# Attention of layers 0 and 2: projections one head group further ahead, in two banks, with a single score bank and a ring of six for q

## The reference

```
x = x + tanh(g_xattn[i]) * xattn_i(layernorm(x), ctx)
x = x + tanh(g_ffn[i])   * ffn_i(layernorm(x))

# xattn of layers 0 and 2, 16 heads of 8:
q = xn @ Wq + bq;  k, v = ctx @ Wk + bk, ctx @ Wv + bv
attn = softmax(q @ k.T * scale  (+ mask * -1e9 in layer 2))
out  = (attn @ v) @ Wo + bo
```

## Time and profile before

| | |
|---|---|
| median of 3 runs | 1286.11 us (1279.64 to 1290.08) |
| the profiled execution | 1285.64 us, span 1283.9 us |
| TensorE busy | 977.4 us, 76% of the span |
| VectorE busy | 771.4 us, 60% |
| ScalarE busy | 571.7 us, 45% |
| GpSimd busy | 393.6 us, 31% |
| mean granted TensorE clock | 0.842 |
| batches of layer 0's attention | about 38 to 125 us of the span |
| batches of layer 2's attention | about 840 to 952 us |

### The profile page before, as it was taken

How to read it: one execution, slowest core, us unless ns; L and a number is a source line. 1 busy time by engine, 2 the same in 40 slices (tenths; PEclk the granted TensorE clock), 3 DMA queues, 4 the chain that set the end, 5 groups by cost and what they waited for, 6 DMA issues and landing times. The chain is left out here.

```text
span 1283.9 us, 17163 instructions
## 1 busy us (share of the span) xinstructions
PE 977.4 (76%) x5366; PEld 731.0 (57%) x5366; DVE 771.4 (60%) x1924; ACT 571.7 (45%) x1101; POOL 393.6 (31%) x519
## 2 busy tenths in 40 slices
PE   2797576698888888488888888478867578883766
PEld 2575354566566665266666666357745357772544
DVE  3687565566766777366666656356765414545674
ACT  1575242355555555155555544156634133321553
POOL 2432002122323232146565656333310132210321
PEclk9899677667777778689999999689978679996887
DMA  4000000000000000000000000100000200000001
GB/s 117 1 2 2 1 1 19 1 18 18 18 18 18 18 9 10 1 1 1 1 1 1 1 1 1 36 1 2 2 19 1 64 2 1 1 1 1 1 1 33
DMA packets 25607, 14.12 MB, mean 11 GB/s; under 512 B 10776, under 2 KB 25007, under 8 KB 25391
## 3 DMA queue, kind: packets, MB, share of 16 engines
q1 hardware_dynamic: 25518, 13.03, 3.8%
HBM read 11.98 MB, written 1.05 MB: 10 GB/s over the span
## 5 line engine op out<-in xcount | busy, mean ns | idle before, releaser
L1470 POOL TENSOR_TENSOR L1f_h<-L1f_h,L1f_gb 128x512 f32<-128x512 f32 (+1 forms) x96 | 152.2, 1588 | 116.5 <-DVE L1f_h L1760 96.7
L718 ACT ACTIVATE L_pt<-bank 128x512 f32<-128x512 f32 x224 | 131.3, 597 | 60.8 <-PE bank L604 56.9
L705 ACT ACTIVATE L_part<-bank,L_bias_ca,const 128x256 fp32r<-128x256 f32 x128 | 68.9, 563 | 111.9 <-PE bank L545 111.9
L406 POOL TENSOR_TENSOR L_kc<-L_kc_all,const 128x256 fp32r<-128x256 f32 x96 | 59.0, 618 | 179.7 <-PE bank L604 127.1
L1760 DVE TENSOR_TENSOR L1f_h<-L1f_a,bank 128x512 f32<-128x512 f32 (+1 forms) x96 | 65.4, 682 | 69.9 <-ACT L1f_a L1600 69.3
L1600 ACT ACTIVATE L1f_a<-bank 128x512 f32<-128x512 f32 (+1 forms) x96 | 57.3, 597 | 111.9 <-PE bank L1525 111.8
L1768 DVE TENSOR_TENSOR L1f_h_lo<-L1f_h,L1f_h_hi 128x512 fp32r<-128x512 f32 (+1 forms) x96 | 88.2, 919 | 11.1 <-ACT L1f_h_hi L1613 11.1
L844 DVE TENSOR_REDUCE L_ms<-bank 128x2 f32<-128x512 f32 x128 | 84.5, 687 | 17.0 <-PE bank L566 16.7
L566 PE MATMUL bank<-L_k,L_q 32*128 32x256 f32 x256 | 73.4, 397 | 12.2 <-DVE L_ms L844 8.9
L830 DVE SCALAR_TENSOR_TENSOR L_q<-bank,L_bias_c,L_part 128x256 fp32r<-128x256 f32 x96 | 46.2, 481 | 58.9 <-ACT L_part L705 57.7
L842 DVE TENSOR_REDUCE L_mc<-bank 128x8 f32<-128x512 f32 (+1 forms) x96 | 65.4, 682 | 24.2 <-PE bank L559 14.8
(11 more groups left out here) (405 smaller groups left out, 2608.9 us busy)
## 6 DMA issues: line engine op xcount, KB each, us to landing
L_raw<-in_L_ffn_w_dram SPq DMA_DIRECT2D x8, 176.0 KB, 2.3
L_raw<-in_L_ffn_v_dram SPq DMA_DIRECT2D x8, 176.0 KB, 2.5
const<-in_const_dram SPq DMA_DIRECT2D x1, 1036.0 KB, 5.0
x<-in_x_dram SPq DMA_DIRECT2D x2, 512.0 KB
L_raw<-in_L_ffn_w_dram SPq DMA_DIRECT2D x8, 128.0 KB, 2.6
L_mask<-in_mask_Bx1xSxS_ff_dram SPq DMA_DIRECT2D x2, 512.0 KB
out_dram<-x SPq DMA_DIRECT2D x2, 512.0 KB
L_raw<-in_L_ffn_w_dram SPq DMA_DIRECT2D x8, 48.0 KB, 2.5
```

What stands on the lines that cost most here:

```text
L705: last = act.activation(part[:, i].bitcast(F32R), b_proj[:, i * S:(i + 1) * S], ACT.Identity, bias=bias_ca[:, i, g:g + 1], scale=pr.c("ak" ...
L718: act.activation(pt[:, g // 2, (g % 2) * NS + i], b_st[(g * NS + i) % 2][:], ACT.Exp, scale=scale).then_inc(sem["exp_done"], 1)
L1470: pool.tensor_tensor(h[0:m, r], h[0:m, r], gb[0:m, gate_slot(c)], ALU.mult).then_inc(sem["h_done"], 1)
```

## The change

For layers 0 and 2 (not `own_keys`):

- `proj` is issued for group g+4 in place of g+3, and alternates between bank 0 and bank 3 (`proj_banks[g % 2]`). It waits for DVE L830 of two groups before, no longer of the group before. `part` is used in two halves in turn.
- Bank 3 was the second score bank. `scores` now has bank 2 alone and waits for the DVE maxima of the group before.
- `q` grows from four slots to a ring of six.
- `scale` and `turn` are issued for batch b+2 in group 3, where they were issued for b+1 in group 0. In `end[3]` the turn stands behind `y(b-1)`. `keys`, `mask_in` and `mask` stay in their places.
- `first` takes on the projection of group 3, `scale(1)` and `turn(1)`.

```diff
-        q = sb("q", [P, NG, S], F32R)
+        RING = NG if own_keys else NG + 2
+        q = sb("q", [P, RING, S], F32R)
+        proj_banks = (b_proj,) if own_keys else (b_proj, b_sc[1])
+        sc_banks = b_sc if own_keys else b_sc[:1]
+        AHEAD = len(proj_banks)
+        def slot(b, g):
+            return (b * NG + g) % RING
 ...
-            + banks("scores", 0, 1) + [("maxima", 0, 0)]
+            + banks("scores", 0, 1) + ([] if own_keys else [("proj", 0, 3), ("scale", 1)]) + [("maxima", 0, 0)] \
+            + ([] if own_keys else [("turn", 1)])
 ...
             if more:
-                begin[0] += [("scale", b + 1), ("mask_in", b + 1)]
-                end[0] += [("turn", b + 1)]
+                if own_keys:
+                    begin[0] += [("scale", b + 1)]
+                    end[0] += [("turn", b + 1)]
+                begin[0] += [("mask_in", b + 1)]
                 end[1] += [("mask", b + 1)]
             if late:
                 ...
                 end[3] += [("y", b - 1)]
+            if not own_keys and b + 2 < B:
+                begin[3] += [("scale", b + 2)]
+                end[3] += [("turn", b + 2)]
 ...
-                for at in group(g + 3):
-                    steps += [("proj", *at), ("keys", *at)]
+                steps += [("proj", *at) for at in (group(g + 3) if own_keys else group(g + 4))]
+                steps += [("keys", *at) for at in group(g + 3)]
 ...
 def proj (TensorE)
-                    need(pe, sem["qk_split"], b * NG + g)
+                    need(pe, sem["qk_split"], b * NG + g - (AHEAD - 1))
-                        o = b_proj[:, i * S:(i + 1) * S]
+                        o = proj_banks[g % AHEAD][:, i * S:(i + 1) * S]
 def scores (TensorE)
-                    need(pe, sem["sc_taken"], b * U + (at + i - 1))
-                    o = b_sc[(at + i) % 2]
+                    need(pe, sem["sc_taken"], b * U + (at + i - (len(sc_banks) - 1)))
+                    o = sc_banks[(at + i) % len(sc_banks)]
 def proj (VectorE)
-                    need(dve, sem["st_done"], b * U + (g + 1) * NS - U)
+                    need(dve, sem["st_done"], (b * NG + g + 1 - RING) * NS)
```

More of the change, by code:

```diff
@@ L558, in scores @@
                             ts = slice(t * P, (t + 1) * P)
-                            last = pe.matmul(o[:, t * S:(t + 1) * S], q[:, g, ts], kc[:, g], start=True, stop=not masked)
+                            last = pe.matmul(o[:, t * S:(t + 1) * S], q[:, slot(b, g), ts], kc[:, g], start=True, stop=not masked)
                             if masked:
@@ L595, in weights @@
                                 continue
-                            pe.matmul(op, keys_of, q[:, g], start=True, stop=False)
+                            pe.matmul(op, keys_of, q[:, slot(b, g)], start=True, stop=False)
                             if masked:
@@ L702, in proj @@
                     act.wait_ge(sem["proj_done"], b * NG + g + 1)
-                    need(act, sem["qk_split"], b * NG + g)
+                    need(act, sem["qk_split"], b * NG + g - (AHEAD - 1))
                     for i in range(2 if own_keys else 1):
-                        last = act.activation(part[:, i].bitcast(F32R), b_proj[:, i * S:(i + 1) * S], ACT.Identity,
+                        last = act.activation(part[:, i if own_keys else g % 2].bitcast(F32R), proj_banks[g % AHEAD][:, i * S:(i + 1) * S], ACT.Identity,
                                               bias=bias_ca[:, i, g:g + 1], scale=pr.c("ak" if i else "aq"))
@@ L827, in proj @@
                     dve.wait_ge(sem["proj_hi"], b * NG + g + 1)
-                    need(dve, sem["st_done"], b * U + (g + 1) * NS - U)
+                    need(dve, sem["st_done"], (b * NG + g + 1 - RING) * NS)
                     for i in range(2 if own_keys else 1):
-                        last = dve.scalar_tensor_tensor((k if i else q)[:, g], b_proj[:, i * S:(i + 1) * S], bias_c[:, i, g:g + 1],
-                                                        part[:, i], ALU.add, ALU.add)
+                        last = dve.scalar_tensor_tensor(k[:, g] if i else q[:, slot(b, g)], proj_banks[g % AHEAD][:, i * S:(i + 1) * S],
+                                                        bias_c[:, i, g:g + 1], part[:, i if own_keys else g % 2], ALU.add, ALU.add)
                     last.then_inc(sem["qk_split"], 1)
@@ L837, in scores @@
                     dve.wait_ge(sem["sc_done"], b * U + (at + i + 1))
-                    bank = b_sc[(at + i) % 2][:]
+                    bank = sc_banks[(at + i) % len(sc_banks)][:]
                     if i == 0:
```

## The result

The changed kernel took 1297.3 us (median of 20 runs, 1283.37 to 1305.81) against 1286.05 us (20 runs, 1269.41 to 1295.88): 11.25 us more. The ratio is 1.0091 with a 95% interval of [1.0063, 1.0119]; it is taken from the fast runs alone (16 of the 20 of the changed kernel), because some executions fall into a slower state. Forecast were 1293 us, or +7.4 on 1285.6, a ratio of 1.0058, in a range of 1282 to 1302. The time lies in the range, on the forecast side and within 1%; the size was too small by some 4 us.

What follows compares the result with a forecast made beforehand. Layer 0 batches were taken as near DVE's 8.30 us floor, layer 2 as paced by TensorE. Moved turns +4.05 and +3.9, edges +0.1 and -0.7, gave +7.4 on 1285.64: 1293 us, range 1282 to 1302.

Steps and rivals of the forecast that it cites:

- deciding term: Turn behind y waits for DVE's L902: +0.81 us per batch in layer 0, +0.78 in layer 2, five times each.
- DVE's account: 8.30 busy: Layer 0 batch counted on DVE: 8.30 busy + 0.51 + 0.34 + 0.13 + 1.03 of waits = 10.31 us.
- the walk: Step-by-step timing of one changed layer 0 batch from the end of `xt_lo`: 10.34 us, against 9.53 before.
- the wait of 0.13 before a second q: Layer 0, group 1: DVE was to wait 0.13 us before that group's q.
- The clock rival: Clock falls at the ten turns, one group at half rate after each: 10 us, 1303; two groups, 1313; 18%.
- signs of being wrong: L526 not waiting for L902, a layer 0 batch under 9.5 us, or the batches' clock column below 0.95.
- the main case: The walked case, with the turn waiting for y and granted clock still 1.00: 1289 to 1298 us, 63%.
- The sum: Layers 0 and 2 together: 4.05 + 3.9 + 0.1 - 0.7 = +7.4 us.
- The term for the edges: First and last batches of layers 0 and 2: +0.1 at the starts, -0.3 and -0.4 at the ends.
- The hidden turn: L902 as early as TensorE's y, turn starts at once: batches 9.31 and 12.5, -2 us, 1284; 14%.
- both waits vanish: Removed waits count fully, 0.8 + 0.66 us per layer 0 batch, 0.65 per layer 2 batch: -15, 1271; 5%.
- The part costed at nothing: Single score bank, other banks, ring and halves of `part`: no cost in the steady batches.

Runs made afterwards that it cites:

- e1: Changed kernel with y(b-1) moved behind the turn of b+2: batches of 9.55 (layer 0) and 12.87 us (layer 2); 1287.71 us, ratio to the kernel before 1.0026.
- e2: Kernel before with only y(b-2) moved directly ahead of turn(b+1): batches of 10.84 and 13.89 us; 1297.19 us, ratio 1.0102.
- e8: Changed kernel with the copy into L_mx written as a one-element reduction: batches of 10.23 and 13.35 us; single run, 1302.96 us.
- e4: Changed kernel with two transposed-input buffers, scale and turn of b+2 in group 0: batches mostly 9.01 to 9.12, and 11.89 us; 1275.32 us, ratio 0.9876.
- e7: e4 with the copy into L_mx written as a one-element reduction: batches of 8.37 and 11.89 us; 1275.04 us, ratio 0.9901 to the kernel before.
- e3: Kernel before with a single score bank in layers 0 and 2: batches of 9.53 and 12.58 us; single run, 1292.1 us.
- e9: Kernel before with e4's two buffers and early turn, L_mx by reduction, no projection ahead: batches of 8.92 and 11.97 us; 1282.47 us, ratio 0.9977.

## Why the prediction was right, and where its size was off

**The deciding term held.** The turn waited for L902 as walked: 1.25 us of TensorE in layer 0 (1.2 said), 0.79 in layer 2 (0.8), DVE 0.95 before `xt_lo` (1.0), DVE's 0.50 before q kept (0.51). Layer 2 was given +0.78 per batch and took +0.78. e1 takes the wait away, and the loss goes but for 0.3 us in layer 2; e2 puts `y` and the turn together with nothing else of the change, and a loss comes, larger than the wait by a second wait of DVE.

**Layer 0 was mis-sized by 0.14.** Its batch was walked to 10.34 and took 10.48. The step that failed is "DVE's account: 8.30 busy", taken over unchanged: the new order makes DVE's copy into L_mx start while GpSimd writes `kc`, where it had started 0.02 us ahead of it, and DVE's busy time became 8.52. e8 shows it: 0.25 us per batch. The rest of the walk was 0.1 too long: in e8 DVE is busy for 8.25 and idle for 1.98 us of a batch, where 8.30 and 2.04 were walked; the wait of 0.13 before a second q did not come. The two errors partly cancel.

**The clock rival was half right.** I gave 18% to a fall at each of ten turns, 10 us. It fell at one: 12.03 in place of 10.48 us, some 1.5 us. So one of the signs of being wrong, a clock column under 0.95, showed in one batch of ten (0.86). That term was missing in the main case. The Trainium skill, "TensorE: Matmul & The Clock Gate", section "A second HAM failure mode: psum-queue depth-cycling", describes a clock that swings with small idle gaps between groups of matmuls; here it fell once and did not swing: the later batches ran at 1.00 with the same gaps and the same cycling through banks.

**The sum, again.** From the first to the sixth `y`, layer 0 took 53.47 us (65.12 to 118.59) and before 47.70 (65.96 to 113.66): +5.8, where 4.05 were said. The difference is the dip (1.5) and four batches that are 0.14 too long, less 0.34 in the last of the five stretches, which took 10.00: no scale follows there, and DVE is busy for only 8.14. Layer 2 took 66.77 (891.41 to 958.18) against 62.89: +3.9, as said. The ends: layer 0 ends 0.2 slower and layer 2 ends 0.3 faster. The starts tell nothing: layer 0 reached its first `y` 0.8 us earlier than before in one profile of the changed kernel and 1.1 later in the other, layer 2 took 62.4 us in one and 57.7 in the other, against 59.8. What the batches and ends explain is thus some +9.5 us, the dip among them, inside the measured interval of +8 to +15. The term for the edges (+0.1 at the starts, -0.7 at the ends) is not confirmed: the ends gave -0.2, the starts can't be read. The rest can't be told from the clock's scatter, and how near the total came to the forecast is in part luck.

**The other rivals.** The hidden turn (14%) did not come: DVE was late, as its starts had said. Of "both waits vanish" (5%), the reason against it was right, since the turn stood next to its use again; e4 gives it a batch and gets a gain, 11.89 and 9.0, and e7 then 8.37.

**The part costed at nothing** was nothing in the steady batches: e3, the single score bank, 9.53 and 12.58, and e1, with all of the banks changed, 9.55 in layer 0.

## What to carry to other kernels

When a step is moved ahead, look at what it now stands behind in a shared bank: a transpose that reuses the bank of an output waits for the slowest reader of that output, and an in-order engine turns this into a wait for all that follows. A wait taken away in front of an engine that is nearly full moves to that engine; count its busy time first, and expect it to change if another engine's timing shifts against it. Where whole runs scatter by 1%, a batch that repeats within one profile tells a few hundredths of a us; what happens at the start of a stage it does not tell.

## What the runs showed of the hardware

A DVE copy from SBUF to SBUF of 16 elements per partition waits for GpSimd's elementwise instruction that is under way: beside the one that writes `kc` it took 0.40 to 0.63 us in place of 0.18 and ended 0.02 to 0.04 us after it. Where the copy started first, even by 0.02 us, it took 0.18. When a reduction did the same work (e7), it took 0.17 us throughout, though seven in layer 0 started while GpSimd wrote `kc`. The trace of the kernel before had one long case outside the walk, a copy of 1.16 us beside GpSimd's 1.28. The Trainium skill, "SBUF — State Buffer", section "Who interferes with whom", says that copies can use a port pair shared with GpSimd, which whoever starts first holds for its whole instruction, and that reductions never do; all of these rows agree.

The same program took spans of 1297.8 and 1286.5 us in two profiles, at mean granted clocks of 0.831 and 0.848, with repeating attention batches equal to 0.02 us. The stages with low clocks make the scatter: layer 1's attention, the same code in all kernels here, took between 318.8 (e9) and 335.0 us (e8).
